# Layer two of a graph network on one Trainium2 core: fetched node rows as two F32R halves, five tiles a turn

## What is computed

```
x = x + layer0(relu(layernorm(x)))        # gated, with an edge network
x = x + relu(layer1(relu(layernorm(x))))
# layer1, for each edge e with source src[e], destination dst[e] and four numbers sh[e]:
#   row   = H[src[e]]                      H = relu(layernorm(x)), one row of 160 per node
#   plane = sh[e][k] * row, k = 0..3       summed over the edges of one dst, then mixed by
#   out   = fixed 160-column weights per k, built from W1..W5, Ws, Wv
```

## Time and profile before

| | us |
|---|---|
| median of 3 runs | 1921.43 |
| lowest and highest | 1919.09, 1923.35 |
| span of the profiled execution (first to last instruction) | 1922.0 |
| PE busy in the span | 1773.5 (92%) |
| DVE busy | 1376.6 (72%) |
| POOL busy | 1405.2 (73%) |
| ACT busy | 179.3 (9%) |

### The profile page before, as it was taken

The page is one execution under the profiler, slowest core; times in us unless marked ns, Lnnn a source line. Parts: engine busy times, 40 slices in busy tenths (PEclk is TensorE's granted clock), DMA queues, the critical chain, the costliest instruction groups (busy, mean ns, idle before and its releaser), DMA issues.

```text
span 1922.0 us, 59005 instructions
## 1 busy us (share of the span) xinstructions
PE 1773.5 (92%) x16922; PEld 1554.1 (81%) x16922; DVE 1376.6 (72%) x2841; ACT 179.3 (9%) x415; POOL 1405.2 (73%) x1498
## 2 busy tenths in 40 slices
PE   8989898989999988889875999999999999999998
PEld 6567676767667676767645899999999999999998
DVE  7888887878787878878878466656656565666654
ACT  5100000010010100000032000000000000000000
POOL 4677777777777777777755777777777777777774
PEclk9999999999999999999987999999999999999999
DMA  7433344333343333333323323223222323223323
GB/s 251 122 103 106 104 105 106 105 105 106 95 114 94 105 105 104 106 105 105 103 77 97 76 73 78 76 72 77 73 76 73 76 72 76 76 73 76 75 74 92
DMA packets 113339, 181.97 MB, mean 95 GB/s; under 512 B 31272, under 2 KB 80720, under 8 KB 112848
## 3 DMA queue, kind: packets, MB, share of 16 engines
q0 software_dynamic: 70272, 120.03, 25.2%
q1 hardware_dynamic: 35592, 55.14, 9.1%
q10 hardware_dynamic: 7112, 2.94, 0.6%
HBM read 170.94 MB, written 7.05 MB: 93 GB/s over the span
## 4 chain that ended last, share of the span: by engine, by line
POOL 43%; PE 26%; issue 18%; ACTq 6%; DVE 4%; DMA 1%; ACT 1%; POOLq 0%; DVEq 0%
POOL g L841 42%; PE sums L1147 8%; PE sums L1132 5%; PE w_ps L1100 5%; ACTq L733 5%; PE hid_ps L1086 3%; PE sums L1157 2%; DVE work L997 1%; ACT work L867 1%; DMA g<-node_table 1%; ACTq L730 1%; DVE work L991 1%; PE w_ps L604 1%; PE sums L576 0%; ACT lin_sb L873 0%
## 5 line engine op out<-in xcount | busy, mean ns | idle before, releaser
L841 POOL DMA_INDIRECT g<-node_table,src x1453 | 1379.4, 949 | 468.4 <-issue 439.1
L1147 PE MATMUL w_ps<-H,work 128*128 128x160 f32 x2900 | 404.3, 299 | 1.5 <-issue 1.5
L1147 PEld LDWEIGHTS w_ps<-H,work 128*128 128x128 f32 x2900 | 398.0, 190 | 1.7 <-issue 1.7
L997 DVE TENSOR_TENSOR work<-w_ps,g 128x384 f32<-128x384 f32 (+3 forms) x693 | 297.4, 456 | 54.0 <-PE w_ps L1100 33.0
L1016 DVE STREAM_TRANSPOSE turned<-sums 128x160 f32<-128x160 f32 x232 | 79.5, 342 | 322.6 <-PE sums L1157 224.5
L1100 PE MATMUL w_ps<-fc_sb,work 64*128 64x224 f32 x1612 | 219.1, 378 | 96.3 <-ACT work L867 59.4
L1132 PEld LDWEIGHTS sums<-work,sel 128*32 128x32 f32 x6448 | 198.5, 111 | 111.1 <-issue 68.2
L1100 PEld LDWEIGHTS w_ps<-fc_sb,work 64*128 64x128 f32 x1612 | 169.5, 191 | 130.6 <-DVE work L991 82.6
L945 DVE TENSOR_TENSOR sel<-mixed,sh 128x896 f32<-128x896 f32 x232 | 251.6, 1084 | 27.6 <-DVE mixed L941 2.1
L1132 PE MATMUL sums<-work,sel 128*32 128x160 f32 x6448 | 246.9, 304 | 1.9 <-DVE work L991 1.0
L1136 PE MATMUL sums<-g,sel 128*128 128x160 f32 x1612 | 238.2, 301 | 9.8 <-DMA g<-node_table,src 9.8
(11 more groups left out here) (103 smaller groups left out, 709.5 us busy)
## 6 DMA issues: line engine op xcount, KB each, us to landing
g<-node_table SPq DMA_DIRECT2D x2304, 0.6 KB
g<-node_table ACTq DMA_DIRECT2D x2304, 0.6 KB
feat<-edge_feat_dram SPq DMA_DIRECT2D x60, 512.0 KB
g<-node_table,src POOLq DMA_INDIRECT x1453
named<-src_rows_dram SPq DMA_DIRECT2D x30, 192.0 KB
X<-x_dram SPq DMA_DIRECT2D x5, 400.0 KB, 6.6
named<-src_rows_dram SPq DMA_DIRECT2D x30, 64.0 KB
sh<-edge_sh_dram SPq DMA_DIRECT2D x1, 1624.0 KB, 9.0
```

Source lines behind the costliest of these rows:

```text
L841: nc.gpsimd.indirect_dma_start(out=g[:, slot(p, u, j), :], out_offset=None, in_=table[layer], in_offset=bass.IndirectOffsetOnAxis(ap=src[: ...
L997: nc.vector.tensor_tensor(blocks(at), w[:, :, 2 * S_CH + j * V_CH:2 * S_CH + (j + 1) * V_CH].unsqueeze(2).to_broadcast([P, n, m, V_CH]), r ...
L1147: last = nc.tensor.matmul(found_at[:, i, 0:D], match[layer][i][:, t, :], H[:, t, :], start=(t == 0), stop=(t == NT - 1))
```

## The change

Only the picked tiles of layer two change, with what is needed for them.

- **Five picked tiles in every turn** (`PICKS`): tile 6 of groups 0, 1 and 2, tile 5 of groups 1 and 3. Of the 806 tiles of layer two 144 are now picked (5 x 28 + 4) and 18 come by row, so 644 are gathered.
- **Node rows as two halves.** A new matrix `split` holds for each node tile 320 columns of type F32R: the row copied to F32R by ScalarE (`scalar_mid`), and the rest, `H` minus that copy, by VectorE (`vector_mid`). `match` is of type F32R too. `find` (L1215) makes 25 products of 128 x 320 in place of 25 of 128 x 160; TensorE needed two records (two loads of weights, two products in the trace) for each of the latter.
- **VectorE joins.** The result has two halves of 160 columns in PSUM. `join` (L1009) adds them with one reduction into `g`; ScalarE's `put` is gone in layer two.
- **ScalarE casts.** The source numbers of four picked tiles are cast at once into PSUM (`cast_early`, L894), those of the fifth into SBUF (`cast_late`, L900), a turn ahead. VectorE's casts L958 are gone in layer two. `named_read`, on which SP's next load of source numbers waits, is now counted by ScalarE.
- **Order.** VectorE's `turn` of layer two moves ahead of `compare`, and `join` comes behind. Ahead of the first group VectorE makes three comparisons in place of one. SP loads the source numbers ahead of its row DMAs of a turn, not behind the first quarter.
- **Memory.** `work`, `feat` and `acc0` become one arena, in which `split` and two of three `match` buffers lie in layer two. The third lies over `H`, which is why VectorE waits for the rows to be stored before layer two.

```diff
+PICKS = ((0, 6), (1, 5), (1, 6), (2, 6), (3, 5))
+MATCH_OF = (0, 1, 2, 0, 1)
+BANK_OF = (0, 1, 2, 3, 1)
+NP = len(PICKS)
+EARLY = NP - 1
...
+        split = nc.alloc_sbuf_tensor_at("split", [P, NT, 2 * D], F32R, offset=arena_at)
+        match = [nc.alloc_sbuf_tensor_at(f"match{b}", [P, NT, P], F32R, offset=at)
+                 for b, at in enumerate((arena_at + 4 * SPLIT, arena_at + 4 * (SPLIT + NPAD), H_at))]
...
+        early_named = hid_ps[:, 0:EARLY * P].rearrange("p (i e) -> p i e", e=P)
+        late_named = arena_part(SPLIT + 2 * NPAD, P)
+        wanted_of = [early_named[:, i, :] for i in range(EARLY)] + [late_named]
...
+                def cast_early(f, nxt):
+                    act.wait_ge(named_in[layer], 16 * f + (16 * nxt + 16))
+                    if nxt:
+                        act.wait_ge(match_done, NP * f + EARLY)
+                    nc.scalar.activation(early_named, named[:, 0:EARLY, :], ACT.Copy).then_inc(named_cast, 1)
...
+                def compare(f, i, nxt, s):
...
+                    dve.wait_ge(named_cast if i < EARLY else late_cast, f + (nxt + 1))
+                    n = NP * nxt + i + LAST_OF[i] + 1
+                    if not (s is not None and s < UNROLL and n <= 0):
+                        dve.wait_ge(found, NP * f + n)
+                    wide = [P, NT, P]
+                    nc.vector.tensor_tensor(match[MATCH_OF[i]][:], wanted_of[i].unsqueeze(1).to_broadcast(wide),
+                                            node_id_sb[:].unsqueeze(2).to_broadcast(wide),
+                                            ALU.is_equal).then_inc(match_done, 1)
+                def join(f, p, i, nxt, s):
...
+                    dve.wait_ge(found, NP * f + (NP * nxt + i + 1))
+                    nc.vector.tensor_reduce(g[:, slot(p, u, j), :], banks[:, BANK_OF[i], 0:2 * D].rearrange("p (h c) -> p c h", h=2),
+                                            AXX, ALU.add).then_inc(found_copied, 1)
...
+                def find(f, i, nxt, s):
...
+                    pe.wait_ge(match_done, NP * f + (NP * nxt + i + 1))
+                    for t in range(NT):
+                        last = nc.tensor.matmul(banks[:, BANK_OF[i], 0:2 * D], match[MATCH_OF[i]][:, t, :], split[:, t, :],
                                                 start=(t == 0), stop=(t == NT - 1))
...
+            act.wait_ge(feat_idle, 1)
+            act.wait_ge(h1_ready, BY_ACT)
+            nc.scalar.activation(split[:, 0:BY_ACT, 0:D], H[:, 0:BY_ACT, :], ACT.Copy).then_inc(upper_ready, 1)
+            act.wait_ge(h1_by_dve, len(by_dve))
+            nc.scalar.activation(split[:, BY_ACT:, 0:D], H[:, BY_ACT:, :], ACT.Copy).then_inc(upper_ready, 1)
...
+            for h, at in enumerate((slice(0, BY_ACT), slice(BY_ACT, NT))):
+                dve.wait_ge(upper_ready, h + 1)
+                last = nc.vector.tensor_tensor(split[:, at, D:2 * D], H[:, at, :], split[:, at, 0:D].bitcast(F32), ALU.subtract)
+            last.then_inc(split_ready, 1)
...
+            dve.wait_ge(split_ready, 1)
+            dve.wait_ge(rows1_out, 16 * len(pieces))
```

More of the change, by code:

```diff
@@ L28 @@
 I32 = mybir.dt.int32
+F32R = mybir.dt.float32r
 ALU = mybir.AluOpType
@@ L640, in edge_layer, with picks_at, exists, fetched @@
             pass_of = {}
[L641 to L658, removed]
-                u, nxt = (o + ahead) % UNROLL, (o + ahead) // UNROLL
[L661 to L666, removed]
-                return u in picks_of(p) and not (own_weights and s is not None and not UNROLL <= s < GROUPS - UNROLL)
-            found_at = sums[:, 0:1, 256:512] if own_weights else banks
+            def picks_at(o, s, ahead):
+                u, nxt = (o + ahead) % UNROLL, (o + ahead) // UNROLL
+                if s is not None and s + ahead >= GROUPS:
+                    return []
+                return [(i, nxt) for i in range(NP) if PICKS[i][0] == u]
+            def exists(i, s):
+                return s is None or s < GROUPS and PICKS[i][1] < tiles_of(s)
+            def fetched(s):
+                return s is None or UNROLL <= s < GROUPS - UNROLL
+            found_at = sums[:, 0, 256:256 + D]
             def tiles_of(s):
@@ L785, in sync_turn @@
                 some = a + (b - a) // 4
+                if not own_weights:
+                    more_rows(sp, f, it)
                 if part == 0:
@@ L922, in stage @@
                         copy(f, 1 if o >= UNROLL else 0)
+                    if not own_weights and (s is None or s < GROUPS - UNROLL):
+                        if o == 0:
+                            cast_early(f, 1)
+                        if o == 2:
+                            cast_late(f, 1)
                     row_part(f, it, o, s, p, e, k)
@@ L1039, in stage @@
                         else:
-                            compare(f, p, e, PICKED[layer][0], 0, 0, True)
-                    if s is None or s < GROUPS:
-                        select(f, it, o, s)
-                        if pick_after(o, s, p, 2):
-                            compare(f, p, e, (o + 2) % UNROLL, *pick_after(o, s, p, 2), s is not None and s + 2 < UNROLL)
+                            for u in range(2):
+                                for i, nxt in picks_at(0, s, u):
+                                    compare(f, i, nxt, s + u)
+                    live = s is None or s < GROUPS
+                    before = None if s is None else s - 1
+                    if live:
+                        select(f, it, o, s)
+                    if not own_weights:
+                        if s is None or 1 <= s <= GROUPS:
+                            turn(f, o - 1, before)
+                        if s == 0:
+                            for i, nxt in picks_at(o, s, 0):
+                                join(f, p, i, nxt, s)
+                        for i, nxt in picks_at(o, s, 2) if live else []:
+                            compare(f, i, nxt, None if s is None else s + 2)
+                        for i, nxt in picks_at(o, s, 1) if live else []:
+                            join(f, p, i, nxt, None if s is None else s + 1)
+                    if live:
                         if s == GROUPS - 2:
@@ L1056, in stage @@
                                 else:
-                                    compare(f, p, e, 2, 0, 1, False)
-                    if s is None or 1 <= s <= GROUPS:
-                        turn(f, o - 1, None if s is None else s - 1)
+                                    match_rows(f)
+                    if own_weights and (s is None or 1 <= s <= GROUPS):
+                        turn(f, o - 1, before)
                     if s == GROUPS:
```

170 lines of the change are left out of this document (103 added, 67 removed).

## The result

| | before | changed |
|---|---|---|
| median of the runs, us | 1921.02 (6 runs, 1918.46 to 1924.18) | 1928.36 (6 runs, 1926.54 to 1932.38) |
| ratio of the times | 1 | 1.0043 (95%: 1.0031 to 1.0055) |
| span of the profiled execution, us | 1922.0 | 1930.6 |

What follows compares the result with a forecast made beforehand. VectorE was taken as the likeliest bound at 28.2 us a turn, level with GpSimd (28.0): from 1038.4, 812.0 us of its work less 1.1 gives 1849.3, plus 16.4 to the end 1865.7, a span of 1866 us; range 1847 to 1908.

Steps and rivals of the forecast that it cites:

- GpSimd's turn: Layer two's gathers: 22.33 a turn at 1.255 us each, 28.0 us a turn, down from 30.5.
- small form: Fifth comparison costs GpSimd 0.64 us each turn: 28.7 us a turn, span 1867, up to 1885; counted within the forecast's 0.55.
- rival (d): Fifth comparison, both operands in SBUF, blocks GpSimd's gathers: by 0.64 us a turn, or wholly (3.4 us, chance 0.04).
- full form: A gather waits for the whole fifth comparison: 3.4 us a turn, 1947 us, slower than before; chance 0.04.
- TensorE's turn: Layer two: five finds of 3.4 us (25 products of 135.8 ns), plus 7.64 and 2.18: 26.8 us a turn.
- the section on the waits: Layer two's turn: comparisons and joins ready before TensorE needs them; casts and row DMAs fit too, costed at nothing.
- Rival (c): Layer two's finds: F32R needs over one pass or weight loads show; TensorE passes VectorE's 28.2 us at 147 ns; chance 0.13.
- the forecast's own case: Layer two paced by VectorE at 27.8 to 28.7 us a turn, giving 1854 to 1880 us; chance 0.55.
- SP and ScalarE at nothing: Layer two: ScalarE's casts and SP's row DMAs and new first load fit in idle time, so cost nothing.
- the sign: A wait of TensorE for DMA in the group by row would show the costing of SP and ScalarE wrong.
- the floor's terms: Layer two's gathers: 59 fewer at 1.255 us, 74.0 us saved; with 17.95 us after the last, span 1848 us.
- the start of VectorE's work in layer two: Subtractions of 4.3 us delay the weights and ScalarE's cast, so VectorE first compares at 1038.4.

## Why the prediction was wrong, point by point

**The step that failed is GpSimd's turn.** The prediction took it as 22.33 gathers of 1.255 us, 28.0 us, and put what the fifth comparison costs GpSimd at nothing, or at 0.64 us in the small form of rival (d). The runs show (d) in its full form: each of the 28 comparisons held one gather, 77.0 / 28 = 2.75 us, GpSimd's turn was 30.65 us and ate the 74.0 us saved. The mechanism and its place stand in the prediction, at 3.4 us a turn and 1947 us, with a chance of 0.04; the misjudgement is that chance. The price was too high since a gather that starts x behind the comparison loses 3.45 + 0.82 - 0.95 - x = 3.32 - x, and x lies anywhere between 0 and 1.25 us, one interval of the gathers: 2.7 us on average.

**The row that misled** was the gather at 1024.96 in the earlier trace rows, read as a gather that ran under L1290 unharmed. It began 0.07 us *before* L1290 (1025.03), and the experiments show that such a gather is through. The row that should have decided is the one behind it, which the prediction did not use:

```profile
1026.21 1.13 POOL L841 DMA_INDIRECT g<-node_table,src  x1 [0.30 <-issue]
```

This gather of the kernel before did start under L1290. L1290 ended at 1025.03 + 1.49 = 1026.52, and 0.82 us later is 1027.34 = 1026.21 + 1.13. Read so, this row gives the delay behind VectorE's instruction and, with the one at 1024.96, the rule of who begins first. The full form could then have been priced at 1848 + 28 x 2.7 = about 1924 us, 4 us under what was measured.

**TensorE's turn** was mis-sized: 26.8 us forecast, 28.4 measured once the other two losses were gone. 125 products at 146.5 ns instead of 135.8 are 1.3 us of it, and 0.3 us is waiting for comparisons, which the section on the waits had put at nothing. Rival (c) named 147 ns as the point from which TensorE passes VectorE, and this is where it ended. The 2.4 ns above the columns were carried over from products that come in two records; nothing in the trace said that a new form has the same excess. With (d) and the late rows gone the time was 1880, not 1866, just at the edge of the forecast's own case (1854 to 1880), though with TensorE as the bound and not VectorE.

**SP and ScalarE at nothing** was wrong, and the prediction had named the sign: a wait of TensorE in the group by row. It cost 1911.5 - 1880.1 = 31 us once the hold was gone. In the changed kernel itself, with its turn of 30.65 us, the wait is there too but short (5.7 us in the stretch, against 19.7); that it cost little there is read from the waits and not measured. ScalarE's busy share of 4% was no argument, for the time that it spends issuing DMAs is not in it (10.81 us for 24 rows).

**Right** were: the floor's terms (59 gathers, 1.255 us each, which close the account above); the start of VectorE's work in layer two, first comparison at 1038.49 for 1038.4 forecast, subtractions 4.39 for 4.3, copies 1.80 + 1.92 for 3.6; and VectorE's instructions, with joins of 0.477 us for 0.41 and comparisons of 3.45 for 3.41. That its turn came to 28.1 us for 28.2 (with the numbers in PSUM and the new table) is in part chance: 26.4 us are work, and the issue in the rest can shrink, as the kernel with 256 columns shows.

```profile
1018.32 1.80 ACT L1309 ACTIVATE split<-H 128x1920 fp32r<-128x1920 f32 x1
...
1023.28 4.39 DVE L1364 TENSOR_TENSOR split<-H,split 128x1920 fp32r<-128x1920 f32 x2
...
1038.49 6.89 DVE L996 TENSOR_TENSOR match<-hid_ps,node_id_sb 128x3200 fp32r<-128x3200 f32 x2 [7.49 <-ACT hid_ps L894]
```

The range, 1847 to 1908, left the full form of (d) out. The forecast had three engines within 1.4 us of each other in a turn, and GpSimd and TensorE each had more to do than was costed.

## What to carry to other kernels

Before moving an operand of a long VectorE instruction from PSUM to SBUF, see whether GpSimd issues indirect DMAs beside it: with both operands in SBUF each such instruction held one gather until it was over, 2.75 us for 3.45, and 25 columns copied to PSUM took all of that away. When a row seems to speak against a rule of exclusion, look at which of the two began first, to the hundredth of a microsecond. When a wait is mended and the time moves less than the wait was long, read the waits again before doubting the mend: here 77 us of hold covered 31 us of late rows, and those covered a TensorE term 1.3 us a turn too small.

## What the runs showed that was not expected

- A gather ends 0.81 to 0.83 us after the VectorE instruction that held it, in all 28 + 57 + 29 cases, and one that began 0.02 us ahead of it was not held. The comparison in turn loses at most 0.06 us to a gather that began first (3.51 against 3.45).
- The hold is for one instruction at a time: cut in four, the same comparison held two gathers by 0.62 and 0.48 us.
- An F32R product takes 13 to 16 ns above its columns at 2.4 GHz (256, 320 and 448 columns), while a record of an F32 product takes 2.4 ns above. Half the weights make it 1 ns shorter.
- Waits of 2.2 to 2.8 us of TensorE were followed by a lower granted clock in five of eight cases, which made such a wait cost up to 1.5 us more.
